# Context turned by 32 by 32 blocks on VectorE instead of by TensorE in a decoder layer kernel

## The reference

```
x = layernorm(x + retention(x))            # ternary weights, decayed cumulative sum over the tokens
q = (x @ Wq + bq)   .reshape(16, 256, 16, 64)       # 16 heads of 64
k = (ctx @ Wk + bk) .reshape(16, 1601, 16, 64)
v = (ctx @ Wv + bv) .reshape(16, 1601, 16, 64)
attn = softmax(q k^T / 8)
x = layernorm(x + (attn v) @ Wo + bo)
x = layernorm(x + mixture(x))              # 8 experts, one per token, with a capacity
```

## Time and profile before

| | us |
|---|---|
| median of 3 runs | 2920.29 (2919.21 to 2920.5) |
| the profiled execution: its own time | 2920.9 |
| its span | 2919.1 |
| busy: PE, PEld | 2709.9, 2289.5 |
| busy: POOL, DVE, ACT | 2124.4, 1979.4, 1718.3 |

### The profile page before, as it was taken

How to read it: one execution, slowest core, us unless ns; L and a number is a source line. 1 busy time by engine, 2 the same in 40 slices (tenths; PEclk the granted TensorE clock), 3 DMA queues, 4 the chain that set the end, 5 groups by cost and what they waited for, 6 DMA issues and landing times.

```text
span 2919.1 us, 70614 instructions
## 1 busy us (share of the span) xinstructions
PE 2709.9 (93%) x28248; PEld 2289.5 (78%) x28248; DVE 1979.4 (68%) x3986; ACT 1718.3 (59%) x3422; POOL 2124.4 (73%) x1708
## 2 busy tenths in 40 slices
PE   5699999999999999999999999999999999997281
PEld 3588888888888888888888888888888888886250
DVE  6667777777777777777777777767777777774104
ACT  2367666666667666667666666667666667663020
POOL 2287787787787787787787778787778787776405
PEclk9699999999999999999999999999999999998595
DMA  3100000000000000000000000000000000000032
GB/s 98 47 9 18 9 20 7 20 9 7 20 9 18 9 20 7 20 9 19 9 20 8 8 20 7 20 9 18 9 20 7 20 9 8 8 9 19 25 94 65
DMA packets 89904, 57.73 MB, mean 20 GB/s; under 512 B 14806, under 2 KB 87211, under 8 KB 89586
## 3 DMA queue, kind: packets, MB, share of 16 engines
q1 hardware_dynamic: 87538, 49.42, 5.9%
q0 software_dynamic: 2048, 3.91, 0.5%
HBM read 44.93 MB, written 8.65 MB: 18 GB/s over the span
## 4 chain that ended last, share of the span: by engine, by line
PE 90%; issue 4%; POOL 3%; DVE 1%; ACT 1%; DMA 0%; POOLq 0%; DVEq 0%; SPq 0%; ACTq 0%
PE ps L1335 26%; PE ps L1366 24%; PE ps L1325 8%; PE ps L1316 4%; PE ps L1317 3%; PE ps L1318 3%; PE ps L1300 3%; PE ps L1301 3%; PE ps L1302 3%; PE ps L1375 3%; PE ps L1384 2%; PE ps L1307 2%; PE ps L1473 1%; PE ps L1480 1%; POOL prob_T L665 1%
## 5 line engine op out<-in xcount | busy, mean ns | idle before, releaser
L620 POOL TENSOR_TENSOR key_sums<-key_sums,prob_T 128x512 f32<-128x512 f32 (+1 forms) x1408 | 1811.1, 1286 | 162.1 <-ACT prob_T L783 1.3
L1013 DVE TENSOR_REDUCE mx<-ps 128x1 f32<-128x400 f32 (+1 forms) x2048 | 1061.4, 570 | 437.5 <-PE ps L1325 379.9
L783 ACT ACTIVATE prob_T<-ps 128x512 f32<-128x512 f32 x1536 | 833.5, 596 | 107.6 <-PE ps L1335 60.0
L1335 PE MATMUL ps<-shift,shift_w 64*128 64x256 f32 (+1 forms) x3328 | 775.1, 281 | 6.6 <-ACT shift L762 6.6
L1335 PE MATMUL ps<-q_hi,k_hi 64*128 64x256 f32 (+1 forms) x3328 | 769.0, 285 | 0.0
L1335 PE MATMUL ps<-q_lo,k_hi 64*128 64x256 f32 (+1 forms) x3328 | 746.1, 278 | 0.0
L1335 PE MATMUL ps<-q_hi,k_lo 64*128 64x256 f32 (+1 forms) x3328 | 745.7, 277 | 0.0
L1366 PE MATMUL ps<-prob_T,v_sb 128*64 128x256 f32 (+1 forms) x6656 | 740.5, 379 | 1.1 <-ACT prob_T L783 1.1
L1366 PEld LDWEIGHTS ps<-prob_T,v_sb 128*64 128x64 f32 (+1 forms) x6656 | 478.0, 137 | 242.1 <-ACT prob_T L783 2.0
L1335 PEld LDWEIGHTS ps<-shift,shift_w 64*128 64x128 f32 (+1 forms) x3328 | 573.2, 180 | 56.0 <-issue 56.0
L1335 PEld LDWEIGHTS ps<-q_lo,k_hi 64*128 64x128 f32 (+1 forms) x3328 | 555.9, 182 | 0.0
(11 more groups left out here) (172 smaller groups left out, 3355.1 us busy)
## 6 DMA issues: line engine op xcount, KB each, us to landing
shift_f<-row_shifts SPq DMA_DIRECT2D x256, 64.0 KB, 2.6
ctx_raw<-in_ctx_dram SPq DMA_DIRECT2D x16, 768.0 KB
row_shifts<-nm_T SPq DMA_DIRECT2D x512, 0.5 KB
tables<-in_L_ffn_W_dram SPq DMA_DIRECT2D x16, 256.0 KB, 3.2
slots_in<-zeros SPq DMA_DIRECT2D x32, 64.0 KB
xs<-in_x_dram SPq DMA_DIRECT2D x8, 256.0 KB, 3.0
xres<-in_x_dram SPq DMA_DIRECT2D x8, 256.0 KB, 3.0
v_sb<-slots_in SPq DMA_DIRECT2D x8, 256.0 KB, 2.7
```

What stands on the lines that cost most here:

```text
L620: op = nc.gpsimd.tensor_tensor(acc[0:rows, :, :], acc[0:rows, :, :], prob_T[0:rows, :, k, :], ALU.add)
L783: nc.scalar.activation(prob_T[:, h, 2 * i - 2:2 * i, :].rearrange("p k t -> p (k t)"), ps[:, bank, :], ACT.Exp).then_inc(ring_act, 1)
L1013: v.tensor_reduce(mx[:, qt, h, c:c + 1], ps[:, at.bank("mx", r, c, qt, h), 0:WID[c]], AX.X, ALU.max).then_inc(ring_dve, 1)
L1335: return mm(ps[0:rows, bank, n * T:n * T + T], keys_part, query_part[lanes, :], start=(step == 0), stop=(step == 3))
```

## The change

For every batch the context is loaded by ten DMAs. Eight of them take 32 of the 128 columns and half of the rows: 800 runs of 128 bytes, laid so that each 32 by 32 block stands in its place with rows and columns still to be exchanged. The last two take the last row (1601 is 50 times 32 and 1). VectorE exchanges rows and columns within all blocks by its transpose (four instructions a batch, of 512, 512, 512 and 96 columns), from ctx_raw to the new ctx_T. ctx_hi and ctx_lo are made from ctx_T, in slot 5 as before. The transposes of PE and their four banks of the ring are gone.

The turning of the next batch's context stands at the end of slots 2, 3 and 4 on DVE. SP issues the loads of a batch in four parts, each after the shift of its slot: in slots 6 and 7 of the batch two before, and in slots 0 and 1 of the batch before. The first context is loaded from ACT's queue near the start of the program, the second by SP once the first is turned. To make room, the three small tiles of the ternary weights lie in the tile of the values.

```
     if kind == "start":
-        for c in range(4):
-            put("dve", "ctx", 0, c)
...
-        if s == 5 and more:
-            for c in range(4):
-                put("dve", "ctx", 8, c)
...
-        ctx_raw = sb("ctx_raw", [P, KT, P])
+        ctx_raw = sb("ctx_raw", [P, TURNED])
+        ctx_T = sb("ctx_T", [P, TURNED])
...
+        def load_context(eng, b, piece):
+            if piece < 8:
+                half, j = piece // 4, piece % 4
+                k0, n = half * (BLOCKS // 2), BLOCKS // 2
+                src = C_IN[b * KEYS + 32 * k0:b * KEYS + 32 * (k0 + n), 32 * j:32 * j + 32]
+                dst = ctx_raw[32 * j:32 * j + 32, 32 * k0:32 * (k0 + n)]
+                eng.dma_start(dst.rearrange("i (k c) -> i k c", c=32), src.rearrange("(k i) c -> i k c", i=32))\
+                    .then_inc(ctx_in, 16)
+            else:
+                row = b * KEYS + KEYS - 1
+                eng.dma_start(ctx_raw[piece - 8:P:32, 32 * BLOCKS:TURNED],
+                              C_IN[row:row + 1].rearrange("a (j c) -> (a j) c", c=32)).then_inc(ctx_in, 16)
...
-                    if s == 5 and at.kind != "last":
-                        next_context(at)
+                    if s >= 6 and at.b + 2 < B:
+                        later_context(at, at.b + 2, s - 6)
+                    if s < 2 and 0 < at.b < B - 1:
+                        later_context(at, at.b + 1, s + 2)
+
+            def later_context(at, b, part):
+                if part == 0:
+                    sp.wait_ge(ctx_turned, 4 * b)
+                for piece in range(part * 2, part * 2 + 2) if part < 3 else range(6, PIECES):
+                    load_context(sp, b, piece)
+
+            sp.wait_ge(ctx_turned, 4)
+            for piece in range(PIECES):
+                load_context(sp, 1, piece)
             turn_shift(Batch("start", 0, B), 0)
...
             copy(wv_hi[:, :], wv_rows).then_inc(w_hi, 1)
+            act.wait_ge(ctx_clear, 1)
+            for piece in range(PIECES):
+                load_context(act, 0, piece)
             act.wait_ge(setup_tr, 1)
...
-                act.wait_ge(ring_full, at.full("ctx", r, c))
-                copy(ctx_hi[:, tiles[0] * P:tiles[0] * P + n], ps[:, at.bank("ctx", r, c), 0:n]).then_inc(ctx_hi_ok, 1)
+            def context_high(b, c):
+                k0, k1 = TURN_CHUNKS[c]
+                act.wait_ge(ctx_turned, b * 4 + c + 1)
+                copy(ctx_hi[:, k0:min(k1, KPAD)], ctx_T[:, k0:min(k1, KPAD)]).then_inc(ctx_hi_ok, 1)
...
+            v.memset(ctx_raw[:, 32 * BLOCKS:TURNED], 0.0).then_inc(ctx_clear, 1)
...
+            def context_turned(b, c):
+                if c == 0:
+                    dve.wait_ge(ctx_in, (b + 1) * PIECES * 16)
+                wait(dve, ctx_lo_ok, b * 4)
+                k0, k1 = TURN_CHUNKS[c]
+                v.transpose(ctx_T[:, k0:k1], ctx_raw[:, k0:k1]).then_inc(ctx_turned, 1)
...
-                v.tensor_tensor(ctx_lo[:, k0:k0 + n], ps[:, at.bank("ctx", r, c), 0:n],
-                                ctx_hi[:, k0:k0 + n].bitcast(F32), ALU.subtract).then_inc(ring_dve, 1)
+            def context_low(b, c):
+                dve.wait_ge(ctx_hi_ok, b * 4 + c + 1)
+                cols = slice(TURN_CHUNKS[c][0], min(TURN_CHUNKS[c][1], KPAD))
+                v.tensor_tensor(ctx_lo[:, cols], ctx_T[:, cols], ctx_hi[:, cols].bitcast(F32), ALU.subtract)\
+                    .then_inc(ctx_lo_ok, 1)
...
                         normalise(at, s - 1)
+                    if 2 <= s < 5 and more:
+                        for c in ((0,), (1,), (2, 3))[s - 2]:
+                            context_turned(at.b + 1, c)
...
-                last = tr(ps[:, bank, n * P:n * P + rows], ctx_raw[0:rows, k, :], ident[0:rows, 0:rows])
...
-            def context_read(at, r):
-                _, count = at.freed("ctx", r, 3)
-                pe.wait_ge(ring_dve, count)
+            def context_read(b):
+                pe.wait_ge(ctx_lo_ok, b * 4 + 4)
```

More of the change, by code:

```diff
@@ L227, in decoder_layer @@
     KPAD = KEYS + 1
+    assert KEYS // 32 % 2 == 0
     assert KT == 2 * (UNITS - 1) + 1 and NJ == SLOTS_A_BATCH
-    K_CHUNKS = [list(range(4 * c, min(4 * c + 4, KT))) for c in range(4)]
+    BLOCKS = KEYS // 32
+    assert KEYS == 32 * BLOCKS + 1
+    TURNED = 32 * (BLOCKS + 1)
+    TURN_CHUNKS = [(c * 512, min(c * 512 + 512, TURNED)) for c in range(4)]
+    PIECES = 10
     NPAIRS = B * NJ
@@ L325, in decoder_layer @@
         wq_rows, wk_rows, wv_rows = (spare[:, n * AD:(n + 1) * AD] for n in range(3))
+        w_rows, w_tmp, w_tern = (spare[:, 3 * AD + n * 4 * P:3 * AD + (n + 1) * 4 * P].rearrange("p (m n) -> p m n", n=P)
+                                 for n in range(3))
         assert 6 * CAP + 8 * NT * E <= 2 * KT * 2 * P
@@ L396, in decoder_layer @@
         ctx_in = sem("ctx_in")
+        ctx_clear = sem("ctx_clear")
+        ctx_turned = sem("ctx_turned")
+        ctx_lo_ok = sem("ctx_lo_ok")
         ctx_hi_ok = sem("ctx_hi_ok")
@@ L532, in _ @@
                 batch(Batch("mid", b, B))
-            at = Batch("mid", B - 2, B)
-            for s in range(NJ):
-                turn_shift(at, s + 1)
+            batch(Batch("mid", B - 2, B))
             batch(Batch("last", B - 1, B))
@@ L807, in batch @@
                         for c in range(4):
-                            context_high(at, NJ, at.b + 1, c)
+                            context_high(at.b + 1, c)
                     if before:
@@ L816, in _ @@
             for c in range(4):
-                context_high(at, 0, 0, c)
+                context_high(0, c)
             for c in range(4):
@@ L1083, in batch @@
                         for c in range(4):
[L1084 removed]
+                            context_low(at.b + 1, c)
                     if s == 1 and at.kind != "first":
@@ L1093, in _ @@
             for c in range(4):
-                context_low(at, 0, 0, c)
+                context_turned(0, c)
+            for c in range(4):
+                context_low(0, c)
             for c in range(4):
@@ L1281, in bank_of @@
                 return banks_of(at, key)[0]
[L1283 to L1288, removed]
-                    last = tr(ps[:, bank, n * P:n * P + rows], ctx_raw[0:rows, k, :], ident[0:rows, 0:rows])
-                last.then_inc(ring_full, 1)
-            def context_read(at, r):
-                _, count = at.freed("ctx", r, 3)
-                pe.wait_ge(ring_dve, count)
+            def context_read(b):
+                pe.wait_ge(ctx_lo_ok, b * 4 + 4)
             def keys(at, r, c):
@@ L1398, in batch @@
                     if s == 6 and more:
-                        context_read(at, NJ)
+                        context_read(at.b + 1)
                     some = value_fills(s) if after else []
@@ L1409, in batch @@
                         project(at)
-                    if s == 5 and more:
-                        for c in range(4):
-                            context(at, NJ, at.b + 1, c)
                     if s > 0 or at.kind != "first":
@@ L1417, in _ @@
             at = Batch("start", 0, B)
-            for c in range(4):
-                context(at, 0, 0, c)
-            context_read(at, 0)
+            context_read(0)
             for c in range(4):
```

22 lines of the change are left out of this document (removed).

## The result

| | before | after |
|---|---|---|
| median of 9 runs each, us | 2920.23 (2918.66 to 2920.63) | 2927.21 (2925.86 to 2928.83) |
| profiled execution's span, us | 2919.1 | 2927.0 |
| first attend starts, us | 156.94 | 159.35 |
| last attend starts, us | 2666.90 | 2676.90 |

The ratio is 1.0026, with a 95% interval of 1.0017 to 1.0036. The kernel is slower by about 0.3%, a small difference, but one that these runs tell from none.

What follows compares the result with a forecast made beforehand. PE, busy 93% of the span, was taken to bound the kernel. The terms summed as 2920.9 - 20.6 + 25.5 + 0 = 2925.8 us for the profiled execution, median 2925.2, with a range of 2897 to 2933.

Steps and rivals of the forecast that it cites:

- The transposes off PE, 1.37 us x 15: In slot 5 the 13 context transposes leave PE, giving 1.37 us a batch in 15 batches, 20.6 us in all.
- DVE's transposes, 0.7 and 0.3, hidden: At the end of slots 2, 3, 4: 0.7 us for 512 columns, 0.3 for 96, hidden in DVE's waits.
- ctx_lo alternates with POOL: In slot 5 ctx_lo, with two SBUF inputs, takes turns with POOL: starts 1.7 us apart, four take about 5.7.
- DVE keeps the port: Rival, chance 0.30: in slot 5 the four ctx_lo run back to back, without turns with POOL; time 2900 us.
- DVE is 2.3 us late: At slot 6's first maximum, ready at 1212.98, DVE comes 2.3 us late, its heads_T ending at 1215.3.
- The ring's slack of 0.64, PE stands in unit 2: In slot 6 the first maximum's PSUM bank leaves 0.64 us of slack, so PE waits 1.7 us in unit 2.
- The start, 0 (-1.5 to +1.5): Before the first attend, ACT's load issues and the first context's turning on DVE together cost 0 us, -1.5 to +1.5.
- The price of an issue: At the start each of ACT's ten load issues takes 0.5 us, 5 us in all, within 7.3 us free.
- the rival: Chance 0.12: ACT's ten issues before w_T hold up the setup, +7.3 us at 1.46 each; time 2932.5.
- The clock's part: At the first context PE, having run less just before, could keep the low clock longer; 0 taken, -1.5 to +1.5 us.
- PE's first token transposes come after 31.5: Sign at the start that the prediction is wrong: these transposes begin later than 31.5 us; PE started at 31.52 before.
- The loads, 0: Context loads, 6408 packets a batch, at most 12.4 us spread over four slots of 19 us, cost 0.

## Why the prediction came out right

The time was 2927.2 against 2925.2 forecast, and the mechanism was the one named: work leaves PE, ctx_lo takes turns with POOL, and DVE's lateness costs more than was gained. That the sum came within 2 us is in part luck, as terms that were missed cancel. Step by step:

- **The transposes off PE, 1.37 us x 15.** Measured 1.36 in slot 5.
- **DVE's transposes, 0.7 and 0.3, hidden.** Measured 0.70 and 0.23, not lengthened by POOL, and free even when doubled.
- **ctx_lo alternates with POOL.** Predicted starts 1.7 us apart and 5.7 for the four; the second came 0.93 after the first, the next two 1.69 and 1.68 apart, and the four took 5.59. (One reading was off without effect: 681 ns in the earlier trace rows is the median of all 64, the shortest of the 48 with 512 columns took 679.) That it is POOL is shown by the run with POOL idle, and that POOL gets its turn between two of DVE's instructions by the run with a single one. The rival "DVE keeps the port" had the price right for what would follow if it were so (2900; 2899.75 with POOL idle).
- **DVE is 2.3 us late.** Measured 2.12.
- **The ring's slack of 0.64, PE stands in unit 2.** The slack is 0.64, as the run with the heads first shows. But the step was incomplete: it took the bank of the maximum for the only link from DVE to PE. The copy of the heads, which waits for heads_T, has a slack of only 0.23 and comes first. That is 0.4 us a batch, 6 us in 15, that the sum lacked. The lateness, taken 0.2 too high, gave half of it back: 1.7 predicted, 1.88 measured, and +7.6 over the batches against +5. heads_T was counted in DVE's chain, but the text never asked who waits for it.
- **The start, 0 (-1.5 to +1.5).** The price of an issue was taken at 0.5 us; on ACT's queue it was 8.65 / 10 = 0.87. But bo_all, 5.3 us later, was ready before the tokens, so that ACT's issues did not hold up the setup by the way that the rival named. The first context was to come about 1.5 us sooner, and it gained 1.7. What was wrong is phase A ahead of it, which the sum took as unchanged: it ended 2.2 us later. Then the low clock lasted longer and cost 1.9. In all the first attend is 2.4 later, outside the bounds. The clock's part was named, but no row bounded its size. The sign "PE's first token transposes come after 31.5" did appear (31.81), by 0.3 us, and 31.5 was the value of before itself, with no room for scatter.
- **The part behind the last attend, not mentioned.** It gave back 2.1 us, which happens to cancel most of the start. By the second profile of before it would be 1.3; why it is shorter stays open.
- **The loads, 0.** Right, in quarters and at once.

## What to carry to other kernels

Moving an operand from PSUM to SBUF looks free and can be the costliest line of a change: ask of each VectorE instruction which of its operands lie in SBUF, and what GpSimd does at that moment. Where the two have to share, the cost is paid once for each instruction, so make few long ones, or put single ones into slots in which VectorE waits anyway. And before pricing a late engine, list everyone who waits for it: the shortest slack decides, and removing that wait alone uncovers the next.

## What the runs showed of the hardware

- While VectorE instructions with two SBUF inputs and GpSimd's adds are both in line, they take turns one by one: about 1.76 us for 0.68 us of work, whether four stand in a row or one by itself (up to 1.84 for 578 columns). Once it has its turn, a long one keeps it: 1602 columns took 2.47 and 2.90 us for 1.83 us of work.
- A tensor_scalar from SBUF to SBUF in fp32 ran at 0.53 ns a column with GpSimd idle, and took 1.49 us for 512 columns beside it. One tensor input isn't enough to be spared.
- The 32 by 32 transpose in fp32 takes 0.70 us for 512 columns and 0.23 for 96, beside GpSimd too.
- Issuing a load of 800 runs of 128 bytes took 0.58 us on SyncE (4.63 for 8). On ScalarE in the first 20 us, with SyncE issuing too, it took 0.49 on average in the first two and 1.01 in the next six.
